# Softmax row sums in a fused attention block: which engine adds them up, and which engine normalises the rows

## The reference

```python
def layernorm(x): return (x - mean(x)) / sqrt(var(x) + 1e-5)
def attn(x):
    q, k, v = heads(x @ Wq + bq), heads(x @ Wk + bk), heads(x @ Wv + bv)
    att = einsum('bhtd,bhsd->bhts', q, k) / sqrt(32)
    att = where(tril(T, T) * (arange(T) % 4 != 3)[None, :] == 0, -inf, att)
    return einsum('bhts,bhsd->bhtd', softmax(att), v) @ Wp + bp
x = x + layernorm(attn(layernorm(x)))
x = x + layernorm(layernorm(x) @ W[idx] + b[idx])
```

## Time and profile before

| | |
|---|---|
| time of 3 runs | 2565.41, 2567.81 (median), 2570.93 us |
| the profiled execution's own time | 2565.07 us |
| its span, first to last instruction | 2563.3 us |
| granted TensorE clock, mean | 0.986 of full speed |
| busy: PE, DVE, ACT, POOL | 94%, 70%, 58%, 56% |
| chain that ended last | PE 59%, DVE 20%, POOL 7%, issue 6%, ACT 4% |

### The profile page before, as it was taken

How to read it: one execution, slowest core, us unless ns; L and a number is a source line. 1 busy time by engine, 2 the same in 40 slices (tenths; PEclk the granted TensorE clock), 3 DMA queues, 4 the chain that set the end, 5 groups by cost and what they waited for, 6 DMA issues and landing times.

```text
span 2563.3 us, 43166 instructions
## 1 busy us (share of the span) xinstructions
PE 2410.8 (94%) x15380; PEld 924.9 (36%) x15380; DVE 1804.7 (70%) x4820; ACT 1494.5 (58%) x2654; POOL 1427.6 (56%) x1318
## 2 busy tenths in 40 slices
PE   4899999998999999999999999999999999999986
PEld 2343333333343333333344343333234433333322
DVE  7767777777477777767567767767738766777764
ACT  5545566556655556557655565665665555565663
POOL 2235465665656365576754637557756454656623
PEclk9899999999999999999999999999999999999998
...
DMA packets 224352, 137.46 MB, mean 54 GB/s; under 512 B 146730, under 2 KB 196618, under 8 KB 224138
## 3 DMA queue, kind: packets, MB, share of 16 engines
...
## 4 chain that ended last, share of the span: by engine, by line
PE 59%; DVE 20%; POOL 7%; issue 6%; ACT 4%; DMA 2%; SPq 1%; ACTq 0%; POOLq 0%; DVEq 0%
PE psO L1198 12%; PE acc L1160 10%; PE acc L1180 9%; PE psU L1215 8%; PE acc L1131 6%; PE acc L1133 6%; PE acc L1132 6%; DVE MP L939 4%; POOL P L717 3%; ACT P L841 3%; DVE acc L935 3%; DVE STA L907 3%; DVE XR L918 2%; PE acc L1184 1%; DVE XB L918 1%
## 5 line engine op out<-in xcount | busy, mean ns | idle before, releaser
L841 ACT ACTIVATE P<-acc,EX 128x512 f32<-128x512 f32 (+2 forms) x1920 | 1076.6, 636 | 476.4 <-PE acc L1180 237.1
L939 DVE TENSOR_REDUCE MP<-acc 128x1 f32<-128x512 f32 (+1 forms) x1088 | 719.4, 679 | 220.3 <-PE acc L1160 217.1
L717 POOL TENSOR_TENSOR P<-P 128x512 f32<-128x512 f32 x546 | 683.7, 1281 | 151.0 <-ACT P L841 150.5
L1160 PE MATMUL acc<-KST,QST 96*128 96x512 f16 (+10 forms) x2112 | 584.0, 335 | 40.5 <-DVE MP L935 22.2
L935 DVE CUSTOM_DVE_ANT_0 acc<-acc,CB 128x96 f32<-128x96 f32 (+7 forms) x1024 | 450.3, 454 | 241.0 <-PE acc L1160 239.4
L1180 PE MATMUL acc<-QST,KST 98*128 98x512 f16 (+2 forms) x1920 | 571.7, 356 | 23.8 <-DVE MP L935 9.3
L1198 PE MATMUL psO<-P,V 128*32 128x512 f32 (+2 forms) x3840 | 464.8, 556 | 11.7 <-ACT P L841 9.3
L1160 PEld LDWEIGHTS acc<-KST,QST 96*128 96x128 f16 x2112 | 192.4, 97 | 393.1 <-issue 108.0
L722 POOL TENSOR_TENSOR SC<-SC 128x512 f32<-128x512 f32 x64 | 82.3, 1286 | 449.7 <-DVE SC L973 449.6
L1180 PEld LDWEIGHTS acc<-QST,KST 98*128 98x128 f16 x1920 | 179.3, 97 | 375.5 <-issue 154.5
L1215 PE MATMUL psU<-P,ONES 128*32 128x512 f32 (+2 forms) x2688 | 300.4, 519 | 0.0
...
## 6 DMA issues: line engine op xcount, KB each, us to landing
QST<-QKH SPq DMA_DIRECT2D x128, 128.0 KB, 3.2
...
KST<-QKH SPq DMA_DIRECT2D x128, 96.0 KB, 2.7
...
```

Of the source, the lines that this page charges most:

```text
L717: e.tensor_tensor(P[:, acc, a, :], P[:, acc, a, :], P[:, buf, a, :], ALU.add).then_inc(g_s, 1)
L841: e.activation(P[:, p_buf[u, g, sb_], a, t0:512], bank(*step)[:, t0:512], ACT.Exp, scale=EX[:, 1:2]).then_inc(a_e, 1)
L939: e.tensor_reduce(maxima(u, g)[:, r, a, ci:ci + 1], bank(*s)[:, 0:n], AX.X, ALU.max).then_inc(v_m, 1)
L1160: i = e.matmul(bank(*s)[:, 0:n], QST[0:96, h, 128 * r:128 * r + 128], KST[0:96, h, c0:c0 + n], start=True, stop=True)
```

## The change

Five things are edited.

1. `on_pe` goes. PE sums only `acc` (or block 0 when j = 0) and the two narrow blocks: 3 buffers in each group. All blocks from 1 to 3j are added: 3, 6 and 9 for j = 1, 2, 3.
2. `ADDS` gives DVE heads 1 to 3 when j = 1, head 3 when j = 2, heads 2 and 3 when j = 3, besides what it had in the last unit.
3. `norm` moves from DVE to ACT (`normer`), except k = 1, 2, 3 of the last unit. ACT needs bias = -mean * rstd: DVE makes -mean in a fourth small instruction of `stats`, ACT multiplies it in a 128x1 instruction and then runs one Identity instruction with bias and scale. rstd now waits for three of the four `stats` instructions.
4. `high` moves from DVE to ACT.
5. The planner has new durations and needs for these; its due times are unchanged.

```diff
-def on_pe(j, sb):
-    return sb >= 3 * j or sb % 3 == 1
 def added(j):
-    return [s for s in range(1, 3 * j) if not on_pe(j, s)]
+    return list(range(1, 3 * j + 1)) if j else []
 def sum_blocks(j):
-    return [s for s in range(j > 0, 3 * j + 1) if on_pe(j, s)] + (["acc"] if j else []) + [3 * j + 1, 3 * j + 2]
+    return (["acc"] if j else [0]) + [3 * j + 1, 3 * j + 2]
...
+    ADDS = ((), (1, 2, 3), (3,), (2, 3))
...
-        self.add("dve", rank, 1000, ("stats", k, u, r), after)
+        self.add("dve", rank, 1060, ("stats", k, u, r), after)
         self.add("gp", rank, 600, ("rstd", k, u, r), [("dve", "stats", k, u, r), ("dve", "consts")])
+        self.add(self.normer(k, u), rank, 455 if self.normer(k, u) == "dve" else 820, ("norm", k, u, r), [("gp", "rstd", k, u, r)])
+    def normer(self, k, u):
+        return "dve" if k and u == self.NU - 1 else "act"
...
-                add("dve", at, 270 if which == "k" else 340, ("high", job), [("act", "evac", job)], [("QKH", ("sp", "spread", job))])
+                add("act", at, 420 if which == "k" else 540, ("high", job), [("act", "evac", job)], [("QKH", ("sp", "spread", job))])
...
-        return "dve" if u == self.NU - 1 and (g == 3 or g == 2 and a > 1) else "gp"
+        return "dve" if a in self.ADDS[u % self.NJ] or u == self.NU - 1 and (g == 3 or g == 2 and a > 1) else "gp"
...
+                elif kind == "norm":
+                    k, u, r = s[1:]
+                    i, o = rows_of(k, u, r)
+                    ac.wait_ge(v_ln, DV["stats", k, u, r])
+                    ac.wait_ge(g_ln, GP["rstd", k, u, r])
+                    e.activation(NM[:, k, 1, r:r + 1], NM[:, k, 0, r:r + 1], ACT.Copy, scale=RR[:, k, 1, r:r + 1]).then_inc(a_n, 1)
+                    ac.wait_ge(a_n, AC[s] - 1)
+                    e.activation(o, i, ACT.Identity, bias=NM[:, k, 1, r:r + 1], scale=RR[:, k, 1, r:r + 1]).then_inc(a_n, 1)
...
+                elif kind == "high":
...
+                    e.activation(QKH[:, at % 2, 0:n], SC[:, 2, 0:n], ACT.Copy).then_inc(a_h, 1)
...
+                    e.tensor_scalar(NM[:, k, 0, r:r + 1], MV[:, k, r, 0:1], -1.0, None, ALU.mult, ALU.bypass).then_inc(v_ln, 1)
...
-                elif kind == "high":
...
-                    e.tensor_copy(QKH[:, at % 2, 0:n], SC[:, 2, 0:n]).then_inc(v_q, 1)
```

More of the change, by code:

```diff
@@ L173, in front @@
             self.moments(0, u, r, at - 1, [("sp", "load_x", u, r)])
-            add("dve", at - 1, 455, ("norm", 0, u, r), [("gp", "rstd", 0, u, r)])
-            self.turn(1, u, r, at, [("dve", "norm", 0, u, r)], used)
+            self.turn(1, u, r, at, [("act", "norm", 0, u, r)], used)
         turned = [("sp", "turn", 1, u, r) for r in range(4)]
@@ L187, in front @@
                              turned + used + [("dve", "wlow", 0 if which == "q" else 1, mt)])
-                add("dve", at, 270 if which == "k" else 340, ("high", job), [("act", "evac", job)], [("QKH", ("sp", "spread", job))])
-                add("gp", at, 870 if which == "k" else 1110, ("rest", job), [("dve", "high", job)])
+                add("act", at, 420 if which == "k" else 540, ("high", job), [("act", "evac", job)], [("QKH", ("sp", "spread", job))])
+                add("gp", at, 870 if which == "k" else 1110, ("rest", job), [("act", "high", job)])
                 add("sp", at, 1950, ("spread", job), [("gp", "rest", job)])
@@ L280, in finish @@
             self.moments(1, u, r, at, [("act", "evac", ("p", u, r))])
-            add("dve", at, 455, ("norm", 1, u, r), [("gp", "rstd", 1, u, r)])
-            add("gp", at, 1228, ("add_x", u, r), [("dve", "norm", 1, u, r), ("sp", "load_r", u, r)])
+            add("gp", at, 1228, ("add_x", u, r), [(self.normer(1, u), "norm", 1, u, r), ("sp", "load_r", u, r)])
             self.moments(2, u, r, at, [("gp", "add_x", u, r)])
-            add("dve", at, 455, ("norm", 2, u, r), [("gp", "rstd", 2, u, r)])
-            self.turn(2, u, r, at, [("dve", "norm", 2, u, r)])
+            self.turn(2, u, r, at, [(self.normer(2, u), "norm", 2, u, r)])
             self.project(("f", u, r), at, 512, 590, [("sp", "turn", 2, u, r), ("dve", "wlow", 4), ("dve", "fold", 2)])
             self.moments(3, u, r, at, [("act", "evac", ("f", u, r))])
-            add("dve", at, 455, ("norm", 3, u, r), [("gp", "rstd", 3, u, r)])
-            add("gp", at, 1228, ("add_y", u, r), [("dve", "norm", 3, u, r)])
+            add("gp", at, 1228, ("add_y", u, r), [(self.normer(3, u), "norm", 3, u, r)])
             add("sp", at, 650, ("store", u, r), [("gp", "add_y", u, r)])
@@ L509, in sandwich_block @@
                                             "whigh": ("w", 4 if s[0] == "whigh" and s[1] < 2 else 1), "exp": ("e", 1),
-                                            "out": ("o", 1), "ohigh": ("o", 1), "shift": ("m", 1), "cast": ("c", 1)}[s[0]]))
+                                            "out": ("o", 1), "ohigh": ("o", 1), "shift": ("m", 1), "high": ("h", 1), "cast": ("c", 1), "norm": ("n", 2)}[s[0]]))
         DV = counted(order.dve, lambda s: {
@@ L513, in sandwich_block @@
             "allmax": ("p", 2), "scales": ("p", (16, 12, 6)[s[-1]] if s[0] == "scales" else 0), "wlow": ("w", 4 if s[0] == "wlow" and s[1] < 2 else 1),
-            "fold": ("f", 17 if s[-1] == 2 else 1), "stats": ("ln", 3), "norm": ("n", 1),
-            "high": ("q", 1), "peak": ("m", 1), "peaks": ("m", 3), "add": ("s", 1), "invert": ("o", 3)}[s[0]])
+            "fold": ("f", 17 if s[-1] == 2 else 1), "stats": ("ln", 4), "norm": ("n", 1),
+            "peak": ("m", 1), "peaks": ("m", 3), "add": ("s", 1), "invert": ("o", 3)}[s[0]])
         GP = counted(order.gp, lambda s: {
@@ L520, in sandwich_block @@
         staged = max(DV[s] for s in (("wlow", 0, 3), ("wlow", 1, 3), ("wlow", 2)))
-        q_job = [s[1] for s in order.dve if s[0] == "high"]
+        q_job = [s[1] for s in order.act if s[0] == "high"]
         q_slot = {s: n for n, s in enumerate(q_job)}
@@ L566, in summed, with normed, rows_of @@
             return (v_s, DV[step]) if order.adder(u, g, a) == "dve" else (g_s, GP[step])
+        def normed(k, u, r):
+            step = ("norm", k, u, r)
+            return (v_n, DV[step]) if order.normer(k, u) == "dve" else (a_n, AC[step])
+        def rows_of(k, u, r):
+            return ((XB[:, r, :], XB[:, r, :]), (YX[:, r, :], YX[:, r, :]), (YX[:, r, :], resid(u, r)),
+                    (resid(u, r), resid(u, r)))[k]
         def scored(u, g):
@@ L694, in _ @@
                     gp.wait_ge(v_c, READY)
-                    gp.wait_ge(v_ln, DV["stats", k, u, r])
+                    gp.wait_ge(v_ln, DV["stats", k, u, r] - 1)
                     e.tensor_tensor(RR[:, k, 1, r:r + 1], RR[:, k, 0, r:r + 1], NHALF[:, :], ALU.pow).then_inc(g_ln, 1)
@@ L698, in _ @@
                     k, u, r = s[1:]
-                    gp.wait_ge(v_n, DV["norm", 0 if k == 1 else 2, u, r])
+                    gp.wait_ge(*normed(0 if k == 1 else 2, u, r))
                     gp.wait_ge(a_c, AC["cast", k, u, r])
@@ L728, in _ @@
                     u, r = s[1:]
-                    gp.wait_ge(v_n, DV["norm", 1, u, r])
+                    gp.wait_ge(*normed(1, u, r))
                     gp.wait_ge(*resid_in(u, r))
@@ L733, in _ @@
                     u, r = s[1:]
-                    gp.wait_ge(v_n, DV["norm", 3, u, r])
+                    gp.wait_ge(*normed(3, u, r))
                     o = resid(u, r)
```

33 lines of the change are left out of this document (16 added, 17 removed).

## The result

The changed kernel takes **2649.4 us** (median of four runs, 2648.6 to 2650.0) where the kernel before takes 2566.6 beside it (four runs): a ratio of **1.032**, with a 95% interval of 1.0304 to 1.0336. It is 83 us slower. The forecast was 2503, in a range that ended at 2590.

A forecast was written before the change was run, and what follows sets the result against it. The prediction took PE, busy 94% of the span, as the bound, with DVE next. Its terms, -124 + 8 - 8 + 36 + 8 + 15 = -65 us, took 2565.1 to 2500, given as 2503 us; range 2436 to 2590.

The forecast's parts named there:

- lock term: Second and third groups of j = 3: DVE's add pairs wait for POOL's adds, 72 pairs x 0.5 = +36 us.
- The sums with what they bring along: 144 sums off PE in j = 1, 2, 3, -124 us; DVE's added work +8; POOL's extra adds in j = 2 +8.
- The rows: Normalisations moved from DVE to ACT: a held norm gone, -8 us, and ACT's new wait for rstd, +15.
- Both signs named for being wrong: Units with j = 3 longer than 220 us, or units with j = 1 not gaining 5 us.
- rival B: POOL and DVE adds lock each other out, about 2.0 us per pair over 72 pairs; slower, 2611 us; chance 0.22.
- DVE's own work: Second group of j = 3: DVE's work, 44.5 us, bounds it against PE's 42.5; 2 us four times, +8 us.
- The held norm: Third group of j = 3: a DVE norm of 5.96 us beside POOL's adds goes, taken as -8 us.
- ACT's wait for rstd: Normalisations on ACT wait for POOL's rstd, with exponentials queued behind; a third of 44 us taken, +15 us.
- POOL when j = 2: Finishing rows in j = 2 units queue behind POOL's extra adds; 2 us per unit, +8 us.
- A: PE's gain is had whole: adds fall into step and ACT's slack absorbs rstd; 2436 us, chance 0.17.
- C: Exponentials on ACT wait behind rstd, 44.2 us or twice that on the path; 2554 us, chance 0.08.
- D: Change does little: PE was full only of work that had time, stalls for maxima replace sums; 2563 to 2573, chance 0.05.

The follow-up runs named there:

- e1: The changed kernel with each of DVE's 546 adds replaced by a one-input max-reduction over the same 128x512 block, about the same work; 2458.4 us, ratio 0.9575.
- e2: The changed kernel with each of DVE's adds replaced by a one-input max-reduction over 4 columns instead of 512; 2451.1 us, ratio 0.9546.
- e3: The kernel before with only the normalisations and rounded copies moved from DVE to ACT, row sums as before; 2548.2 us, ratio 0.9925.
- e8: The kernel before with only the normalisations moved to ACT; rounded copies stay on DVE, sums as before; 2555.6 us, ratio 0.996.
- e5: The kernel before with normalisations and copies on ACT, 48 fewer PE sums, no DVE adds outside the last unit, POOL adding instead; 2573.7 us, ratio 1.0032.
- e11: The kernel before with normalisations and copies on ACT; for j = 1, 2 three PE sums, head 3 added by DVE in the sums' PSUM bank; 2529.0 us, ratio 0.9856.

## Why the prediction was wrong

**What bounds the kernel.** Right: PE was the bound, and taking 144 sums off it pays as long as nothing else gets in its way (e1, e2). The sum without its lock term is -65 - 36 = -101, thus 2467 us; with the lock taken out the chip ran 2458, 9 us from it. But this is luck in part, for two misses cancel. The sums with what they bring along, -124 + 8 + 8 = -108, measured -90 (e1 against e3). The rows, -8 + 15 = +7, measured -19 (e3).

**DVE beside POOL: the step that failed.** It was the term "72 pairs x 0.5 = +36 us". It measured 191: 76 in the two groups that it was charged for, the second and third of j = 3, and 115 where the sum had nothing. Both signs named for being wrong came true: units with j = 3 at 236.8 us (77.3 + 54.1 + 55.3 + 50.1), over 220, and no gain for j = 1. That the engines would hold each other, which the forecast shared with rival B, was right; three things about its size were not.

- *The wait of a pair.* I took 0.5 us, from the one delayed add of the earlier trace rows. Those rows were the nearest, but of a single group, the third of the last unit, with ten adds on each of the two engines where the changed kernel has eighteen in every group of j = 3. The groups of j = 3 have 18 adds each in 20.6, 22.9, 21.6 and 25.5 us of DVE's time, so 1.0, 1.3, 1.1 and 1.6 us of wait per pair, over its own 1.28. Over the whole kernel it is 0.89 (243 us in 273 pairs). The break-even that I gave for B, 1.4 us per pair, was for 72 pairs; with all of them it lies far lower.
- *Where it counts.* I charged the second and third group of j = 3 only, for their full DVE. Between the changed kernel and e1 lie 119 us in j = 3, over all its groups, and 74 in j = 1 and 2. DVE's slack there is a share over the stretch; a pair that is late by 2 us between two maxima holds PE at once, as in the timeline at 1860.76. An average of 76% hid this in the way that the prediction warned of for PE.
- *The other side.* POOL's adds were held too, 110 us, by which P buffers and rstd come later; no term had this. And PE pays twice: after a stall of 2.77 us its next `pv` took 1.94 us, not 1.07. PE's busy time is 69 us longer than in e1 (2361.7 against 2292.4) with the same instructions, at a mean clock of 0.967 against 0.985.

**DVE's own work, +8:** 7 in all (e1 against e2), but not where it was put. The prediction had DVE full in the second group of j = 3, 44.5 us against PE's 42.5. In e1 that group lasts 42.8 us with DVE busy 39.7, and e2 takes only 0.4 us more off it. The number is luck.

**The held norm, -8, and ACT's wait for rstd, +15:** the sum of both was +7, and the part of the change that makes them measured -19 (e3), the copies included. The normalisations brought 10 (e8). A likely reason is that the 44 us for which DVE had sat waiting for rstd were worth more there, ahead of PE's maxima, than the 34.7 that ACT waits in e3: I had priced the new wait and not the end of the old one, nor the rest of the held time that norms and copies had on DVE. No run separates these. The norm costs ACT 0.81 + 0.29 = 1.11 us where I had 1.02:

```profile
L796 ACT ACTIVATE YX<-YX,NM,RR x60: 812/813/817, 163.3 to 2431.5; 128x512 f32<-128x512 f32 x60
```

**POOL when j = 2, +8:** not separated. e1 has 172.2 us for that unit, where 168 were forecast: 4 us more. e5 shows for j = 1 what POOL's bursts can cost; whether +8 was right for j = 2 is open.

**The rivals.** A (2436) would have needed the adds to fall into step; without a lock the kernel comes to 2458. C is out by e3, D by the result: PE's sums were real time (90 us between e1 and e3). B, at 0.22, was the case in its outcome, and its own figure, 2611, was still low by 38. Its wait of 2.0 us per pair was above the 1.0 to 1.6 measured; what it lacked were the other pairs, POOL's held time and PE's clock. Its picture of DVE waiting out POOL's run, taken from the norm of the earlier trace rows, did not come true for the adds: none waits for more than one POOL instruction.

**What stays open.** Whether POOL's queue or DVE's copies keep e11 from its 2495 was not tried, nor what one score bank is worth by itself, nor what makes the norm and L971 wait out a whole run of POOL's where an add waits for one instruction, nor whether a different split of heads would do better with the accumulator in PSUM.
